# Four graph layers on Trainium2: another order of the same operations on five engines, and other PSUM banks

## The reference

```
for layer in (L0, L1, L2, L3):
    h = max(layernorm(x), 0)
    x = x + layer(h)
L0: g = h @ W (256 -> 128 and two logit columns); softmax over neighbours of
    leaky_relu(e_i + e_j); concat(attention @ g, g)
L1: deg * (h @ Wi + b) + adj @ (h @ Wj)
L2: q, k, v = h @ Wq, Wk, Wv; 8 heads of 32; masked softmax(q k^T); @ v; @ Wo + bo
L3: as L0 with 256 output features, attention alone
```

## Time and profile before

| | |
|---|---|
| three runs | 1173.5, 1175.25 (median), 1176.16 us |
| the profiled execution | 1172.01 us, its span 1170.2 us |
| busy share of the span | PE 93%, ACT 93%, DVE 90%, POOL 82% |
| mean granted TensorE clock | 0.981 |
| SP's queue | 80.8% of what 16 DMA engines can take in the span |

### The profile page before, as it was taken

The page is one execution under the profiler, slowest core; times in us unless marked ns, Lnnn a source line. Parts: engine busy times, 40 slices in busy tenths (PEclk is TensorE's granted clock), DMA queues, the critical chain, the costliest instruction groups (busy, mean ns, idle before and its releaser), DMA issues.

```text
span 1170.2 us, 39812 instructions
## 1 busy us (share of the span) xinstructions
PE 1089.8 (93%) x15256; PEld 917.1 (78%) x15256; DVE 1050.3 (90%) x2975; ACT 1087.6 (93%) x3209; POOL 957.3 (82%) x1734
## 2 busy tenths in 40 slices
PE   3689999999999999999999999999999999999865
PEld 3577888888888888888888888888888888888752
DVE  4489999999999999999999999999999999999861
ACT  3589999999999999999999999999999999999862
POOL 3789888888888888888888888888888888887521
PEclk9899999999999999999999999999999999999895
DMA  5258998889888989888998889889889978997761
GB/s 146 46 108 134 163 171 157 143 166 167 149 153 164 164 147 154 163 164 133 173 163 153 152 164 164 136 164 167 159 141 167 160 149 153 168 163 127 133 129 48
DMA packets 575933, 173.33 MB, mean 148 GB/s; under 512 B 539648, under 2 KB 575744, under 8 KB 575744
## 3 DMA queue, kind: packets, MB, share of 16 engines
q1 hardware_dynamic: 574976, 170.46, 80.8%
q10 hardware_dynamic: 768, 0.33, 0.1%
HBM read 19.73 MB, written 16.78 MB: 31 GB/s over the span
## 4 chain that ended last, share of the span: by engine, by line
ACT 52%; PE 22%; DMA 13%; DVE 5%; POOL 4%; issue 2%; SPq 0%; DVEq 0%; POOLq 0%
DMA h_t<-h_rows 8%; PE ps L399 5%; PE ps L401 5%; PE ps L400 5%; ACT ps L1059 4%; DMA mix_t<-mix_rows 3%; ACT ps L1065 3%; ACT ps L1071 3%; ACT ps L1076 2%; ACT relu L1107 2%; ACT relu L977 2%; ACT relu L980 2%; ACT head_hi L1081 2%; ACT agg_hi L1035 2%; ACT relu L1104 2%
## 5 line engine op out<-in xcount | busy, mean ns | idle before, releaser
L399 PE MATMUL ps<-w_hi,h_t 128*128 128x258 f16 (+2 forms) x768 | 188.8, 258 | 28.1 <-DMA h_t<-h_rows 26.0
L401 PE MATMUL ps<-w_hi,h_t 128*128 128x258 f16 (+2 forms) x768 | 188.2, 257 | 0.0
L400 PE MATMUL ps<-w_lo,h_t 128*128 128x258 f16 (+2 forms) x768 | 188.1, 256 | 0.0
L399 PE MATMUL ps<-w_hi,agg_hi 128*128 128x256 f16 x512 | 139.1, 272 | 1.8 <-DVE agg_lo L783 1.8
L401 PE MATMUL ps<-h_t,w_lo 128*128 128x256 f16 x512 | 139.6, 273 | 0.0
L400 PE MATMUL ps<-h_t,w_hi 128*128 128x256 f16 x512 | 139.6, 273 | 0.0
L399 PE MATMUL ps<-h_t,w_hi 128*128 128x256 f16 x512 | 139.6, 273 | 0.0
L401 PE MATMUL ps<-w_hi,agg_lo 128*128 128x256 f16 x512 | 138.8, 271 | 0.0
L400 PE MATMUL ps<-w_lo,agg_hi 128*128 128x256 f16 x512 | 138.8, 271 | 0.0
L399 PEld LDWEIGHTS ps<-w_hi,h_t 128*128 128x128 f16 x768 | 75.4, 98 | 44.6 <-DMA h_t<-h_rows 31.6
L399 PE MATMUL ps<-v_hi,head_t_hi 128*128 128x33 f16 x1024 | 84.6, 178 | 11.1 <-issue 10.5
(11 more groups left out here) (189 smaller groups left out, 5052.4 us busy)
## 6 DMA issues: line engine op xcount, KB each, us to landing
x<-in_x SPq DMA_DIRECT2D x64, 256.0 KB, 3.2
out<-x SPq DMA_DIRECT2D x64, 256.0 KB, 2.3
h_t<-h_rows SPq DMA_TRANSPOSE x192, 3.6
head_t_hi<-head_hi SPq DMA_TRANSPOSE x64, 5.1
head_t_lo<-head_lo SPq DMA_TRANSPOSE x64, 4.4
mix_t<-mix_rows SPq DMA_TRANSPOSE x64, 3.1
w_f<-in_w_o SPq DMA_DIRECT2D x1, 256.0 KB, 3.3
w3t_f<-in_w_t SPq DMA_DIRECT2D x1, 256.0 KB, 3.5
```

The costliest lines, as they stand in the source:

```text
L399: pe.matmul(o, lh, rh, start=start, stop=False)
L400: pe.matmul(o, lh, rl, start=False, stop=False)
L401: return pe.matmul(o, ll, rh, start=False, stop=stop)
```

## The change

Every operation stays, with its shape and operands. Changed are the five `slot(at)` lists, the banks of the 22 results, and with these the waits: a wait stands where, by the new order, it is first needed. In the new lists many pieces carry a part number that is one lower than before (the logits and softmax of layers 0 and 3, the head exponentials, `norm1`, `norm2`, `cast_query`, `cast_key`), and `move0` one that is higher.

```diff
-        s0_ps = ps[7]
+        s0_ps = ps[5]
-        sh0_ps = ps[1]
+        sh0_ps = ps[5]
-        s3_ps = ps[7]
+        s3_ps = ps[4]
...
             def store_x(g):
-                sp.wait_ge(update3_0_done, g + 1)
+                sp.wait_ge(update3_1_done, g + 1)
...
             def slot(at):
                 at(0, load_x)
-                at(7, move3)
+                at(1, move0)
                 at(5, move_heads_hi)
                 at(5, move_heads_lo)
                 at(3, move2)
-                at(0, move0)
+                at(6, move3)
                 at(5, move_out)
                 at(7, store_x)
...
             def gat_sum0(g):
                 pe.wait_ge(keep_probs0_done, g + 1)
+                if g >= 4:
+                    pe.wait_ge(split_out_0_done, g - 3)
...
             def gat_sum3(g):
                 pe.wait_ge(keep_probs3_done, g + 1)
+                if g < graph_groups - 6:
+                    pe.wait_ge(keep_probs0_done, g + 7)
...
             def slot(at):
-                at(2, aggregate_0)
-                at(7, logit_rows3)
-                at(1, gat_sum0)
-                at(4, head_scores)
+                at(2, message_0)
                 at(5, head_sum_1)
                 at(5, head_sum_0)
-                at(2, message_0)
-                at(7, turn_probs3_0)
-                at(7, turn_probs3_1)
+                at(1, turn_probs0_0)
+                at(1, turn_probs0_1)
                 at(2, message_1)
                 at(7, gat_sum3)
+                at(1, gat_sum0)
                 at(4, make_value)
...
+                at(3, make_query)
+                at(0, feat0)
+                at(1, aggregate_0)
+                at(1, aggregate_1)
+                at(0, logit_rows0)
+                at(3, head_scores)
```

More of the change, by code:

```diff
@@ L752, in update0_0, with update0_1 @@
             def update0_0(g):
+                dve.scalar_tensor_tensor(x[g % XBUF][:, 0, 0:F0], s0_ps[:, 0 * (1 + F0) + 1:1 * (1 + F0)], inv0[g % 2][:, 0:1], x[g % XBUF][:, 0, 0:F0],
+                                         ALU.mult, ALU.add).then_inc(update0_0_done, 1)
+            def update0_1(g):
                 if g == 0:
@@ L781, in split_agg_0 @@
             def split_agg_0(g):
+                if g == 0:
+                    lo_part("o", COL_WO, D)
                 dve.wait_ge(keep_agg_0_done, g + 1)
@@ L912, in update3_1 @@
+            def update3_1(g):
                 dve.scalar_tensor_tensor(x[g % XBUF][:, 1, :], s3_ps[:, 1 * D:2 * D], inv3[g % 2][:, 1:2], x[g % XBUF][:, 1, :],
-                                         ALU.mult, ALU.add)
+                                         ALU.mult, ALU.add).then_inc(update3_1_done, 1)
             def slot(at):
-                at(3, update1_1)
-                at(3, update1_0)
-                at(5, split_head_0)
+                at(3, stats2_0)
                 at(3, stats2_1)
-                at(3, stats2_0)
+                at(5, split_head_3)
@@ L930, in slot @@
+                at(5, split_value)
+                at(2, split_agg_0)
                 at(1, row_max0)
-                at(6, stats3_1)
-                at(4, split_query)
-                at(6, mean_var3)
-                at(4, split_key)
+                at(4, head_max_0)
+                at(4, head_max_1)
                 at(2, split_agg_1)
-                at(5, split_value)
-                at(1, inv_sum0)
-                at(2, split_agg_0)
-                at(7, row_max3)
-                at(1, update0_0)
@@ L953, in slot @@
                 at(5, split_out_0)
+                at(4, split_head_0)
+                at(2, update1_0)
+                at(1, inv_sum0)
+                at(7, update3_0)
+                at(1, update0_1)
+                at(1, update0_0)
+                at(1, stats1_1)
+                at(1, stats1_0)
+                at(7, update3_1)
                 at(1, mean_var1)
-                at(4, head_max_1)
-                at(7, update3_1)
-                at(7, update3_0)
+                at(2, update1_1)
@@ L1028, in keep_agg_0, with keep_agg_1 @@
                 act.activation(agg_hi[g % 2][:, 0, :], ag0_ps[:, :], ACT.Copy).then_inc(keep_agg_0_done, 1)
+            def keep_agg_1(g):
+                act.wait_ge(aggregate_1_done, g + 1)
+                act.activation(agg_hi[g % 2][:, 1, :], ag1_ps[:, :], ACT.Copy).then_inc(keep_agg_1_done, 1)
                 if g == 0:
@@ L1137, in slot @@
             def slot(at):
-                at(5, head_exp_3)
-                at(5, head_exp_2)
-                at(5, head_exp_1)
-                at(5, keep_head_3)
-                at(5, keep_head_1)
-                at(5, keep_head_2)
-                at(2, norm1_1)
-                at(1, keep_feat0)
-                at(2, norm1_0)
-                at(5, keep_value)
-                at(4, cast_query)
-                at(1, leaky0_1)
-                at(1, leaky0_0)
-                at(3, norm2_0)
-                at(3, norm2_1)
-                at(4, cast_key)
-                at(7, keep_feat3_0)
+                at(6, norm3_1)
+                at(6, norm3_0)
+                at(7, keep_probs3)
                 at(1, expo0_0)
                 at(1, expo0_1)
-                at(2, keep_agg_1)
-                at(7, keep_feat3_1)
+                at(4, head_exp_0)
+                at(0, norm0_0)
+                at(4, keep_head_0)
                 at(1, keep_probs0)
-                at(2, keep_agg_0)
-                at(7, leaky3_1)
-                at(7, leaky3_0)
-                at(0, norm0_0)
-                at(6, norm3_0)
-                at(0, norm0_1)
-                at(7, expo3_0)
-                at(7, expo3_1)
-                at(4, head_exp_0)
-                at(6, norm3_1)
-                at(4, keep_head_0)
-                at(5, keep_out_1)
-                at(7, keep_probs3)
-                at(5, keep_out_0)
+                at(5, keep_out_1)
+                at(5, keep_out_0)
+                at(0, norm0_1)
+                at(4, head_exp_1)
+                at(4, head_exp_3)
+                at(4, head_exp_2)
+                at(4, keep_head_3)
+                at(4, keep_head_1)
+                at(4, keep_head_2)
+                at(3, cast_key)
+                at(6, keep_feat3_0)
+                at(6, keep_feat3_1)
+                at(1, norm1_1)
+                at(1, norm1_0)
+                at(4, keep_value)
+                at(6, leaky3_0)
+                at(6, leaky3_1)
+                at(2, norm2_1)
+                at(2, norm2_0)
+                at(3, cast_query)
+                at(6, expo3_0)
+                at(0, keep_feat0)
+                at(6, expo3_1)
+                at(1, keep_agg_0)
+                at(0, leaky0_0)
+                at(0, leaky0_1)
+                at(1, keep_agg_1)
             run(slot)
@@ L1291, in slot @@
             def slot(at):
+                at(7, rows_lo3)
+                at(3, add_deg_bias)
+                at(5, add_out_bias)
+                at(1, rows_hi0)
+                at(1, rows_lo0)
+                at(2, add_eps1)
+                at(2, negate_mean1)
+                at(2, power1)
+                at(2, shift1)
                 at(3, add_eps2)
```

272 lines of the change are left out of this document (125 added, 147 removed).

## The result

| | before | after |
|---|---|---|
| median | 1174.38 us (4 runs, 1172.4 to 1176.16) | 1204.9 us (4 runs, 1195.0 to 1208.72) |
| the profiled execution | 1172.01 us | 1204.52 us |
| mean granted TensorE clock | 0.981 | 0.979 |

The ratio is 1.0247, with an interval of 1.0183 to 1.0311. The kernel got slower, as forecast, but by 30 us where 8 were forecast, and 1204.9 lies outside the range of 1162 to 1193.

The account below looks back on a forecast made before the run. The prediction took ACT, at 16.71 us a slot, as the bound, with two loops through SP's queue adding losses. 1172.0 + 11 (+0.19 in 57 slots) - 2 = 1181, raised by 1 to 1182 us; range 1162 to 1193.

Parts of the forecast that it names:

- ACT's 16.71 a slot: Sum of ACT's 36 pieces in one slot, which the changed kernel can't go under.
- Heads loop: Store, load, transpose, heads high and low, then PE and DVE work to the next store: X + 6.45 us.
- X: Time from the store to the landing of heads low: mean 10.25 us before, 10.0 to 10.25 forecast.
- The terms of message_0, `gat_sum0` and DVE's tail: Changes to the work between heads low's landing and the next store: -1.31, +0.44 and +1.22 us.
- Move loop: Loop through the transpose behind store and load: 12.4 us without the landing, so `move0` may take 4.3 instead of 4.76.
- The larger of the two excesses counts: Loss per slot is the larger excess of X or the move's landing over its bound: 0.34 to 0.41 us.
- The rival in which the losses add: Late heads also delay the next slot's `move0`, so both excesses sum: 1189 to 1193 us, chance 0.13.
- X itself: its SP issues have the same sizes in the same order: Transfers from store to heads low keep their landings, so mean X is 10.0 to 10.25 us.
- The count over before's landings: Larger excess per slot over 54 slots of the kernel before, with the new bounds: 0.34 to 0.41 us, against 0.18.
- PE cools down: PE's clock falls in longer waits; given no chance of its own.
- Filling and draining: First and last slots of the program, the last with a little less to do: -2 us, with ±6 as bounds.
- The train gets shorter: Transfers from the store on meet an empty queue, X falls to 9.5, both loops come free: about 1163 us, chance 0.32.

Follow-up runs that it names:

- e9_both_lock_late: Changed kernel with update3_1 earlier on DVE, load_x behind the heads transfers, 25 idle PE instructions a slot and 84 once at the start: 1159.18 us.
- e1_tail: Changed kernel with DVE's update3_1 moved right behind update3_0, both ahead of inv_sum0: 1160.96 us.
- e6_lock_early: Changed kernel with 25 idle PE instructions a slot (512 in all) and 19 once at the start: 1169.34 us.
- e7_lock_late: Changed kernel with 25 idle PE instructions a slot (512 in all) and 84 once at the start: 1222.57 us.
- e2_load: Changed kernel with load_x moved from between the store and move0 to behind move_heads_lo, for the next group: 1164.86 us.
- e8_before_tail: Kernel before with update1_1 and update1_0 moved ahead of update3_0 on DVE, so its store waits 0.68 us longer: 1193.48 us.

## Why the prediction was right in direction and wrong in size

Point by point, by its own terms:

- *ACT's 16.71 a slot:* right. In e9_both_lock_late every slot is 16.71 to 16.72.
- *Heads loop, X + 6.45, bound 10.25:* right, 6.54 and 10.17. The terms of message_0, `gat_sum0` and DVE's tail are right in their sum (+0.44, where they gave +0.35); no run took them one by one. e1_tail takes 1.38 off the 6.53 and wins 44 us. The forecast's sign, DVE waiting at L755 for `gat_sum0`, showed only three times in 200 to 1000 us (total, times, longest):

```profile
DVE inv L755 <- PE ps L467: 3.6, 3, 1.5
```

- *Move loop, 12.4 without the landing, bound 4.3:* right, 12.39. A third of the slots was to wait for `move0`. This is PE's wait at `feat0` in 200 to 1000 us (total, times, longest), all of it on the transpose of L338; it stands in 25 of the 46 slots there. `move0` or the load sets the length of 17 of the 52 slots, a third:

```profile
PEld ps L394 <- DMA h_t<-h_rows: 30.8, 25, 2.3
...
PE ps L394 <- DMA h_t<-h_rows: 23.8, 20, 2.0
```

- *The larger of the two excesses counts:* right. Over after's own landings and with the forecast's own bounds it gives 0.71 a slot. The rival in which the losses add is not what happened; 1205 is beyond it for another reason. The load's loop, which I had left out, adds less than 0.01 to this, since `move0` is late whenever the load is.
- *"X itself: its SP issues have the same sizes in the same order", so mean X 10.0 to 10.25, and `move0`'s landings those of `move3` before:* this is the step that failed. The count over before's landings gave 0.34 to 0.41; over after's, 0.71. 0.30 to 0.37 times 57 are 17 to 21 us of the 23 us between forecast and result. Same sizes in the same queue don't have the same landings. PE's instruction blocks share the DMA engines, and where they fall depends on how far PE has come in its list when the store leaves. Before, one block in 54 slots began 1.0 to 3.2 us behind the store; in after 15 in 52 did. Locked early (e6_lock_early) the same order loses 0.23 a slot, under the forecast's 0.34 to 0.41; locked late (e7_lock_late) 1.07. SP's wait for `keep_head_2`, which was to shorten X by 0.2 if it went, did go (no such wait is left in after), and X rose all the same. One slip in the sum: with both bounds 0.1 tighter the count over before's landings gives at most +0.29, not +0.31.
- *PE cools down, no chance of its own:* it did, in three slots of the 52 (207.56, 627.05 and 801.12), which are 19.5 to 20.3 long. Windows around one, the clock being the third number from the end:

```profile
806.00:812.00 6.00, 5.13 (x104) 3.85 (x101) 5.91 (x16) 5.74 (x18) 5.36 (x13) 1.00 1.03 176
814.00:818.00 4.00, 4.00 (x53) 3.24 (x50) 3.23 (x10) 2.44 (x9) 3.02 (x4) 0.57 0.34 66
818.00:822.00 4.00, 4.00 (x35) 3.60 (x34) 3.11 (x12) 3.53 (x11) 1.19 (x3) 1.00 0.36 70
```

and the chain there:

```profile
811.50 0.11 PE ps L394
...
811.83 1.73 issue
813.56 0.18 PE ps L394
...
815.52 0.21 PE ps L394
```

PE waited 1.73 us for the heads; between 814 and 818 it then ran wide matmuls every 0.21 instead of 0.11 us, at 1.2 GHz. In the three slots the store came 7.96 to 8.21 behind the landing instead of 6.54. 1.5 us three times over 52 slots is 0.09 a slot, 5 us in all: with 0.71 it makes the measured 0.80.
- *Filling and draining, -2:* about -1.
- *The train gets shorter (faster, 0.32):* no. Mean X rose to 10.70 instead of falling under 9.8. The premise was half right: `mix_t` did land 0.2 us behind the store's issue instead of 1.8, as a mean, but X didn't get shorter by it: even with the blocks locked early its mean is 10.42. The rate of DMA transposes that the Trainium skill gives (DMA: Bandwidth & Descriptors, section Latency and other measured facts) would give an X near 9, by the estimate made there; no run's mean reaches it, the least being the 9.8 of e2_load, where the load is gone from the train.

What stays open: why some waits for the heads bring the clock down and others don't. The three after which it fell were of 1.47, 1.47 and 1.73 us; waits of 1.48 (in the slot of 609.24) and 1.63 (in that of 978.10) at the same place did nothing, so the length of the wait alone doesn't decide. Open too is why four runs of after spread over 14 us where those of before spread over 4, and by which path a block of instructions stops a whole train of transfers.

## What to carry to other kernels

Count the slack of every loop through a transfer, the load's too, against the late landings and not the median: here 1.4 us more of it in the heads' loop won 44 us (e1_tail), 0.68 us less cost 19 (e8_before_tail), and the cure was to put the piece that frees the store first. Landings measured in one order are no input for another, as soon as something else on the DMA engines (here the instruction stream of an engine with some 500 instructions a slot) moves against them; give the estimate a second case in which every slot has a late one. Where an order is laid out by adding up durations to the last tenth, give the transfers a margin first.

## What the runs showed that I had not expected

- PE's instruction stream comes in packets of 16 KB, one for 256 instructions, each of which takes 0.9 to 2.3 us. In after the load that meets one takes 4.2 to 5.7 us, where it has a median of 3.2 otherwise: 1 to 2.5 us more.
- Where the number of PE instructions in a slot isn't a multiple of 256, the delay comes and goes with a period (10 slots for 487). With 512 it stands still, and 65 idle instructions once at the start decide between 1169 and 1223 us.
- Idle waits on PE, 25 in a slot, cost nothing that shows in a slot of 16.71.
